# One subtraction of a fused transformer layer, issued by VectorE in place of GpSimd

## The chip, the core and the metric

The kernel is one program on one core of one Trainium2 chip. Its time is device microseconds (us) from the launch of the program to its end, as the chip reports it. Engines are named as the profile names them: PE is TensorE, PEld its weight loads, DVE VectorE, ACT ScalarE, POOL GpSimd, SP SyncE.

## What is computed

The reference is one layer with adaptive layer norm on a batch of 4 sequences of 1024 rows of 256 numbers: attention, then a routed feed-forward block. The part that the change touches is the last product of the feed-forward block.

```python
h = _layernorm(x) * (1 + ca) + sa
x = x + ga * attention(h)                  # 16 query heads, 4 key heads, causal
h = _layernorm(x) * (1 + cb) + sb
# feed-forward on h:
routed = sigmoid(h @ w_router + b_router) > 0.5
v = rmsnorm(h, norm1_w) @ wv + bv
g = h + v @ wo
h2 = rmsnorm(g, norm2_w)
mlp = (silu(h2 @ w_gate) * (h2 @ w_up)) @ w_down      # inner width FF = 704
x = x + gb * where(routed, g + mlp, h)
```

## The kernel before

The program handles the four sequences one after the other, but the work of neighbouring sequences is interleaved: a hand-written list of step names, ORDER, gives one common order of all steps, and each engine runs those steps of the list that are its own, in that order. An engine never takes a later step ahead of an earlier one. Steps that depend on each other over engines are tied by semaphores, one for each kind of step: a step raises the semaphore of its kind when it is done, and whoever needs it waits for the count. Where ORDER carries a digit behind a PE step, it is the PSUM bank which that step takes; eight banks are shared by all steps, and a PE step also waits until the former holder of its bank has been read out.

The feed-forward block works on pairs of row tiles (256 rows, four pairs to a sequence) and on inner blocks of 128. The 704 inner columns are five full blocks and one of 64, in three groups of two blocks: group 0, the middle group 1 (blocks 2 and 3), and group 2. For each pair and group the steps are

- gate and up on PE (lines 792 to 794), each into a bank;
- sil on ACT (L1001, or L1003 and L1004 for group 2): silu of gate;
- fft on DVE (L1255, or L1257 and L1259 for group 2): product of sil and up, in float32, into one of two buffers of 128x512;
- ffhi on ACT (L1015, or L1017 and L1018): the product rounded to the short format in which PE multiplies fast, the high word;
- the low word, the product less its high word, into fflo. For groups 0 and 2 it is step fflo on DVE (L1267; L1270 and L1272). For the middle group it is step ffl, one instruction of 128x512 on POOL (L564).

Then step down on PE (L581 to L583, 809, 810) multiplies the inner blocks with w_down in three passes: high by high, high by low, low by high. Before block 2 it waits for ffl, the low words of the middle group. Step sum (L1278) on DVE reads the result, and step fin on POOL (L573, L574) applies the gate and adds the residual.

Other steps that the text speaks of: hT, hhi and hlo transpose the normed rows on PE (L756), take the high words on ACT (L969) and the low words on DVE (L1226); a is the product with the fused v and router weights on PE (L581 to L583 with W1hi); route (L1236, L1237, L1239) on DVE reads it; h2T (L775) transposes for gate and up; max and mxr are the row maxima of the scores (PE L684, DVE L1165); ytm (L1189 to L1194) on DVE normalizes attention's output, and ynT (L736) on PE transposes it; rs1, rs2, rstd2 on POOL are inverse square roots (L481, L482); norm1 on POOL is L542, pmask L549.

There are 16 middle groups, one for each pair of each sequence. On the waiting side, these lines matter: the wait of down, and that of fft, which may write its buffer again only when the low word of two groups earlier is done.

```python
for f in range(FB):
    if f == GROUPS[LO_P][0]:
        wait("ffl", j + 1)
    elif f == GROUPS[NG - 1][0]:
        wait("fflo", j * (NG - 1) + 2)
```

Of the kernel before, what the change touches and what calls it, by code (L numbers as in the profile page):

```python
# [6 lines left out]
F32 = mybir.dt.float32  # L7
F32R = mybir.dt.float32r
BF16 = mybir.dt.bfloat16
ALU = mybir.AluOpType  # L10
# [51 lines left out]
NG = 3  # L62
# [5 lines left out]
GROUPS = [(0, 1), (2, 3), (4, 5)]  # L68
LO_P = 1
# [137 lines left out]
def adaln_layer(nc, x, Wq, bq, Wk, bk, Wv, bv, Wo, bo, w_router, b_router, n1, f_wv, f_bv, f_wo, n2,  # L207
                w_gate, w_up, w_down, c_in, wmod, rope_cos, rope_sin, out):
    ctx = ExitStack()
    with ctx:  # L210
# [99 lines left out]
        fft = sb("fft", [P, 2, CH])  # L310
# [9 lines left out]
        ffhi = sb("ffhi", [P, 2, NF, PAIR_T], F32R)  # L320
        fflo = sb("fflo", [P, 2, FB, PAIR_T], F32R)
# [34 lines left out]
        S = {n: sem("s_" + n) for n in N} | dict(setM=s_setM)  # L356
        N |= dict(setM=0)

        def flat(ap):
            return ap.rearrange("p k n -> p (k n)")  # L360
# [96 lines left out]
        @block.gpsimd  # L457
        def _(pool):
            pool.memset(ident[:], 0.0)
            pool.memset(mask_qk[:], 0.0)  # L460
            pool.memset(expo[:], -0.5)
            pool.memset(eps_ln[:], LN_EPS)
            pool.memset(eps_rms[:], RMS_EPS).then_inc(s_const, 1)
            pool.wait_ge(s_const, 1)
            pool.affine_select(out=ident[:], in_=ident[:], compare_op=ALU.not_equal, fill=1.0, base=0,
                               pattern=[[-1, P]], channel_multiplier=1)
            pool.affine_select(out=mask_qk[:], in_=mask_qk[:], compare_op=ALU.is_ge, fill=NEG, base=0,
                               pattern=[[-1, P]], channel_multiplier=1).then_inc(s_const, 1)
            pool.wait_ge(s_const, 2)
            pool.tensor_copy(ident_b[:], ident[:]).then_inc(s_const, 1)  # L470
            chained = [0]

            def then(i):

                i.then_inc(S["pchain"], 1)
                chained[0] += 1
                pool.wait_ge(S["pchain"], chained[0])

            def rsqrt(dst, src, eps, done):

                then(pool.tensor_tensor(dst, src, eps, ALU.add))  # L481
                pool.tensor_tensor(dst, dst, expo[:, 0:dst.shape[1]], ALU.pow).then_inc(done, 1)  # L482

            for kind, b, n, _ in STEPS:
                two = slice(2 * n, 2 * n + 2)
                ring = slice(2 * n % TPC, 2 * n % TPC + 2)

                def wait(name, k):
                    pool.wait_ge(S[name], b * N[name] + k)

                def earlier(name, k):
                    if b > 0:
                        pool.wait_ge(S[name], (b - 1) * N[name] + k)

                def over_two(row):
                    return row.unsqueeze(1).to_broadcast([P, 2, C])

                if kind == "pzero":
                    pool.memset(V[:], 0.0)
                    pool.memset(stk[:], 0.0).then_inc(s_const, 1)  # L500
                    pool.wait_ge(s_const, C_ZERO - 1)
                    pool.memset(stk[:, :, H:2 * H, QK:QKM], 1.0)
                    pool.memset(V[:, :, :, D:D + 1], 1.0).then_inc(s_const, 1)
                elif kind == "gmod":
                    pool.wait_ge(s_setM, M_MOD)
                    rows = modr.rearrange("b (v n) -> b v n", v=4)
                    gates = rows[:, 0:4:3, :]
                    pool.tensor_scalar(rows[:, 2, :], rows[:, 2, :], 1.0, 1.0, ALU.mult, ALU.add)
                    then(pool.tensor_scalar(gsgn, gates, 0.0, 2.0, ALU.is_ge, ALU.mult))
                    then(pool.tensor_scalar(gsgn, gsgn, 1.0, -1.0, ALU.mult, ALU.add))  # L510
                    then(pool.tensor_tensor(gabs, gsgn, gates, ALU.mult))
                    then(pool.tensor_scalar(gabs, gabs, 3.0e38, 0.25, ALU.min, ALU.max))
                    pool.tensor_tensor(gates, gsgn, gabs, ALU.mult).then_inc(s_gmod, 1)
                elif kind == "gw1":
                    pool.wait_ge(s_setM, M_W1 + 1)
                    pool.tensor_tensor(flat(W1lo[:]), flat(w1_st[:]), flat(W1hi[:]).bitcast(F32), ALU.subtract
                                       ).then_inc(s_w1, 1)
                elif kind == "gprep":

                    pool.wait_ge(s_setA, 2 * n + 3)  # L520
                    for src, k, blk, cols in pieces[n]:
                        hi = guhi[:, k, blk, cols]
                        i = pool.tensor_tensor(gulo[:, k, blk, cols], src.rearrange(
                            "p (f n) -> p f n", n=hi.shape[2]), hi.bitcast(F32), ALU.subtract)
                    i.then_inc(s_setG, 1)
                elif kind == "gwd":

                    pool.wait_ge(s_setA, 2 * PIECES + 2)
                    pool.tensor_tensor(wdlo[:], wd_st, wdhi[:].bitcast(F32), ALU.subtract).then_inc(s_setG, 1)
                elif kind == "rstd1":  # L530
                    wait("stats", n + 1)
                    earlier("norm1", (n + 1) * TPC)
                    ts = slice(n * TPC, (n + 1) * TPC)
                    then(pool.tensor_scalar(nmean[:, ts], mv1[:, ts, 0], -1.0, 0.0, ALU.mult, ALU.add))
                    rsqrt(rstd1[:, ts], mv1[:, ts, 1], eps_ln[:, ts], S["rstd1"])
                elif kind == "norm1":
                    wait("rstd1", n // TPC + 1)
                    if n >= TPC:
                        wait("xT", (n - TPC) // 2 + 1)
                    else:  # L540
                        earlier("xT", (NT + n - TPC) // 2 + 1)
                    pool.tensor_scalar(xn[:, n % TPC, :], xres[:, b % NX, n, :], nmean[:, n:n + 1], rstd1[:, n:n + 1],  # L542
                                       ALU.add, ALU.mult).then_inc(S["norm1"], 1)
                elif kind == "pmask":

                    u = DIAG[n]
                    wait("exp", 2 * (u + 1))
                    block_ = PT[:, u % 2, :, 0:P]
                    pool.affine_select(out=block_, in_=block_, compare_op=ALU.is_ge, fill=0.0, base=0,  # L549
                                       pattern=[[0, H], [1, P]], channel_multiplier=-1).then_inc(S["pmask"], 1)  # L550
                elif kind == "rstd2":
                    wait("x1", n + 1)
                    rsqrt(rstd2[:, two], mv2[:, two, 1], eps_ln[:, two], S["rstd2"])
                elif kind == "rs1":
                    wait("ms1", n + 1)
                    rsqrt(rs[:, 0, two], ms[:, 0, two], eps_rms[:, two], S["rs1"])
                elif kind == "rs2":
                    wait("ms2", 2 * n + 2)
                    rsqrt(rs[:, 1, two], ms[:, 1, two], eps_rms[:, two], S["rs2"])
                elif kind == "ffl":  # L560
                    m = n * NG + LO_P
                    wait("ffhi", m + 1)
                    blocks = slice(GROUPS[LO_P][0], GROUPS[LO_P][1] + 1)
                    pool.tensor_tensor(flat(fflo[:, n % 2, blocks, :]), fft[:, m % 2, :],  # L564
                                       flat(ffhi[:, n % 2, blocks, :]).bitcast(F32), ALU.subtract).then_inc(S["ffl"], 1)
                elif kind == "fin" and (b, n) == (B - 1, NJ - 1):
                    continue
                elif kind == "fin":
                    wait("sum", 2 * n + 2)
                    if n == 0:  # L570
                        pool.wait_ge(s_gate[b % 2], 16 * (b // 2) + 16)
                    z = zbuf[:, (b * NJ + n) % Z_PAIRS]
                    then(pool.tensor_tensor(z, z, over_two(gate_b[:, b % 2, :]), ALU.mult))  # L573
                    pool.tensor_tensor(xres[:, b % NX, two, :], xres[:, b % NX, two, :], z, ALU.add  # L574
                                       ).then_inc(S["fin"], 1)
# [446 lines left out]
        def _(dve):  # L1022
# [34 lines left out]
            for kind, b, n, _ in STEPS:  # L1057
                def wait(name, k):
                    dve.wait_ge(S[name], b * N[name] + k)
# [186 lines left out]
                elif kind == "fft":  # L1246
# [9 lines left out]
                    else:  # L1256
# [2 lines left out]
                        i = dve.tensor_tensor(fft[0:FR, n % 2, PAIR_T:CH], sil[FR:P, n % 2, PAIR_T:CH],  # L1259
                                              of("gate", b, n)[FR:P, PAIR_T:CH], ALU.mult)  # L1260
                    i.then_inc(S["fft"], 1)
                elif kind == "fflo":
                    j, g = n // (NG - 1), (0, NG - 1)[n % (NG - 1)]
                    m = j * NG + g
# [58 lines left out]
```

## Time and profile before

| what | value |
|---|---|
| median of 3 runs | 465.63 us |
| lowest and highest run | 465.51 and 466.37 us |
| span of the profiled execution | 466.8 us |
| granted clock of PE, mean of the span | 0.990 |
| PE busy | 437.2 us, 94% of the span |
| DVE busy | 353.9 us, 76% |
| ACT busy | 308.4 us, 66% |
| POOL busy | 182.2 us, 39% |

The profile is of one execution, with a span from its first to its last instruction of 466.8 us; the profile gives no other time of that execution. That span is 1.2 us over the median of the three timed runs, so differences are formed inside the profile and then put on the median. The clock was full but for short stretches at the start and the very end.

### The profile page before, as it was taken

The numbers are of one execution on the slowest core, as the hardware profiler recorded it, in microseconds if no ns is written. First come the engines' busy times: TensorE is split into PE (matmuls) and PEld (weight loads), VectorE is DVE, ScalarE is ACT, GpSimd is POOL, SyncE is SP. The second block draws the span as 40 slices with busy tenths as digits, with TensorE's granted clock in tenths as the row PEclk, the third lists the DMA queues.
The fourth block names the chain that finished last, engine by engine and source line by source line (L and its number), as shares of the span: only waits on it lengthen the run. The fifth ranks groups of instructions, "written<-read, shape, count | busy, mean of one in ns | idle before, by whom it ended". The sixth has DMA issues, their size and how long they took to land. (4 is left out here: it accounts for less than half of the span.)

```text
span 466.8 us, 9486 instructions
## 1 busy us (share of the span) xinstructions
PE 437.2 (94%) x3320; PEld 371.8 (80%) x3320; DVE 353.9 (76%) x796; ACT 308.4 (66%) x640; POOL 182.2 (39%) x262
## 2 busy tenths in 40 slices
PE   5887979888989999999999999999999999999996
PEld 5674545686587688997858999999898798999995
DVE  4579968788989488898855889888885766578565
ACT  2298578775588887527697764676768698645441
POOL 6376527410246220214827404523243333325622
PEclk9999899999999999999999999999999999999998
DMA  7921030000000100020021000000010000000001
GB/s 192 333 93 51 3 97 1 2 1 3 0 3 11 43 2 0 2 70 1 27 86 24 2 1 24 1 26 5 20 51 9 24 22 2 25 1 24 22 25 46
DMA packets 16576, 16.04 MB, mean 34 GB/s; under 512 B 4233, under 2 KB 14926, under 8 KB 16530
## 3 DMA queue, kind: packets, MB, share of 16 engines
q1 hardware_dynamic: 16530, 15.44, 10.8%
q8 instruction: 28, 0.46, 0.4%
q14 instruction: 18, 0.15, 0.1%
HBM read 11.09 MB, written 4.21 MB: 33 GB/s over the span
## 5 line engine op out<-in xcount | busy, mean ns | idle before, releaser
L792 PE MATMUL banks<-gTh,guhi 128*128 128x256 f32 x352 | 101.2, 287 | 0.0
L794 PE MATMUL banks<-gTh,gulo 128*128 128x256 f32 x352 | 98.8, 281 | 0.0
L793 PE MATMUL banks<-gTl,guhi 128*128 128x256 f32 x352 | 98.7, 280 | 0.0
L937 ACT ACTIVATE PT<-banks 128x1024 f32<-128x1024 f32 (+3 forms) x96 | 74.5, 810 | 29.8 <-PE banks L708 24.4
L792 PEld LDWEIGHTS banks<-gTh,guhi 128*128 128x128 f32 x352 | 66.4, 189 | 1.6 <-issue 0.7
L1165 DVE TENSOR_REDUCE mxp<-banks 128x2 f32<-128x1024 f32 (+3 forms) x56 | 61.9, 1141 | 6.4 <-PE banks L684 3.9
L793 PEld LDWEIGHTS banks<-gTl,guhi 128*128 128x128 f32 x352 | 66.5, 189 | 0.3
L794 PEld LDWEIGHTS banks<-gTh,gulo 128*128 128x128 f32 x352 | 66.4, 189 | 0.0
L684 PE MATMUL banks<-QKT 128*128 128x512 f32 (+3 forms) x192 | 49.9, 368 | 6.8 <-ACT QKT L915 3.4
L708 PE MATMUL banks<-QKT 128*128 128x512 f32 (+3 forms) x192 | 50.9, 369 | 0.9 <-ACT PT L937 0.4
L708 PEld LDWEIGHTS banks<-QKT 128*128 128x128 f32 x192 | 30.3, 190 | 23.3 <-issue 21.2
L581 PE MATMUL banks<-wdhi,ffhi 128*128 128x256 f32 x160 | 46.0, 287 | 0.0
L573 POOL TENSOR_TENSOR zbuf<-zbuf,gate_b 128x512 f32<-128x512 f32 x15 | 19.6, 1305 | 66.4 <-DVE zbuf L1278 66.4
L582 PE MATMUL banks<-wdlo,ffhi 128*128 128x256 f32 x160 | 45.1, 282 | 0.0
L583 PE MATMUL banks<-wdhi,fflo 128*128 128x256 f32 x160 | 45.1, 282 | 0.0
L684 PEld LDWEIGHTS banks<-QKT 128*128 128x128 f32 x192 | 29.6, 193 | 13.9 <-issue 7.2
L549 POOL TENSOR_SCALAR_AFFINE_SELECT PT<-PT 128x512 f32<-128x512 f32 x32 | 21.1, 660 | 49.7 <-ACT PT L937 49.5
L720 PE MATMUL banks<-PT,V 128*32 128x512 f32 (+3 forms) x384 | 38.6, 495 | 1.7 <-POOL PT L549 1.6
L481 POOL TENSOR_TENSOR rs<-ms,eps_rms 128x2 f32<-128x2 f32 x32 | 7.6, 239 | 70.1 <-ACT sq L974 51.1
L915 ACT ACTIVATE QKT<-banks 64x512 fp32r<-64x512 f32 (+1 forms) x48 | 26.6, 590 | 10.5 <-PE banks L673 10.1
L1001 ACT ACTIVATE sil<-banks 128x512 f32<-128x512 f32 x32 | 18.7, 594 | 22.3 <-PE banks L794 21.5
L564 POOL TENSOR_TENSOR fflo<-fft,ffhi 128x512 fp32r<-128x512 f32 x16 | 20.9, 1304 | 31.4 <-ACT ffhi L1015 31.4
(178 smaller groups left out, 1093.4 us busy)
## 6 DMA issues: line engine op xcount, KB each, us to landing
xres<-in_L_attn_x SPq DMA_DIRECT2D x8, 512.0 KB, 4.4
out_x<-xres SPq DMA_DIRECT2D x16, 256.0 KB, 2.1
wm_st<-in_L_wmod SPq DMA_DIRECT2D x1, 1024.0 KB, 7.9
modB<-mod_scratch SPq DMA_DIRECT2D x4, 256.0 KB, 3.4
wg_st<-in_L_ffn_w_gate SPq DMA_DIRECT2D x1, 704.0 KB, 5.0
wu_st<-in_L_ffn_w_up SPq DMA_DIRECT2D x1, 704.0 KB, 6.2
xres<-in_L_ffn_w_down SPq DMA_DIRECT2D x1, 640.0 KB, 5.7
wm_st<-in_L_wmod SPq DMA_DIRECT2D x1, 512.0 KB, 6.2
```

The source lines that it names most:

```text
L581: pe.matmul(o, hi, whi, start=first, stop=False)
L582: pe.matmul(o, hi, wlo, start=False, stop=False)
L583: return pe.matmul(o, lo, whi, start=False, stop=last)
L684: i = pe.matmul(o[:, e, m * kn:(m + 1) * kn], QKT[:, q, qt * P:(qt + 1) * P], QKT[:, 2 + 2 * q + e, k0:k0 + kn], start=(m == 0), stop=not ...
L708: i = pe.matmul(o[:, e, 0:CH - q0], QKT[:, 2 + 2 * q + e, j * P:(j + 1) * P], QKT[:, q, c * CH + q0:(c + 1) * CH], start=True, stop=True)
L720: i = pe.matmul(o[h * 2 * D:(h + 1) * 2 * D, q0:CH], V[:, j, h, :], PT[:, n % 2, h, 0:CH - q0], start=(j == 0), stop=(q0 == CH - P), skip_ ...
L792: pe.matmul(out_, guhi[:, k, blk, :], gh, start=(m == 0 and k == 0), stop=False)
L793: pe.matmul(out_, guhi[:, k, blk, :], gl, start=False, stop=False)
L794: i = pe.matmul(out_, gulo[:, k, blk, :], gh, start=False, stop=(m == len(blocks) - 1 and k == KB - 1))
L915: i = act.activation(QKT[rows, to, cols].rearrange("p q (t n) -> p q t n", t=2), o[rows, q:q + 2], ACT.Copy)
L937: act.activation(PT[:, u % 2, 2 * q:2 * q + 2, 0:CH - q0], both("prob", b, n)[:, :, 0:CH - q0], ACT.Exp, scale=float(D) ** -0.5).then_inc( ...
L1165: dve.tensor_reduce(dst, both("max", b, n)[:, :, 0:len(at) * kn].rearrange("p e (m k) -> p e m k", k=kn), AX.X, ALU.max).then_inc(S["mxr"], 1)
```

## The change

The subtraction of the middle group's low words has the same operands, the same semaphores and the same place in ORDER. It is taken out of POOL's program and put into DVE's.

```diff
@@ block.gpsimd @@
-                elif kind == "ffl":
-                    m = n * NG + LO_P
-                    wait("ffhi", m + 1)
-                    blocks = slice(GROUPS[LO_P][0], GROUPS[LO_P][1] + 1)
-                    pool.tensor_tensor(flat(fflo[:, n % 2, blocks, :]), fft[:, m % 2, :],
-                                       flat(ffhi[:, n % 2, blocks, :]).bitcast(F32), ALU.subtract).then_inc(S["ffl"], 1)
@@ block.vector @@
+                elif kind == "ffl":
+                    m = n * NG + LO_P
+                    wait("ffhi", m + 1)
+                    blocks = slice(GROUPS[LO_P][0], GROUPS[LO_P][1] + 1)
+                    dve.tensor_tensor(flat(fflo[:, n % 2, blocks, :]), fft[:, m % 2, :],
+                                       flat(ffhi[:, n % 2, blocks, :]).bitcast(F32), ALU.subtract).then_inc(S["ffl"], 1)
```

Six lines fewer stand ahead of DVE's code after the change, so its lines carry numbers lower by six (L1257 becomes L1251); the moved instruction is L1260. Two places of DVE's program show what stands around it. The first is the first sequence's first pair, some 138 us into the execution. DVE's rows before the change (in brackets the semaphores that a row waits for):

```order
L1221 SCALAR_TENSOR_TENSOR hbuf<-hbuf,rstd,modB 128x256
L1226 TENSOR_TENSOR hTl<-banks,hTh 128x512 [waits s_hhi]
L1257 TENSOR_TENSOR fft<-sil,banks 128x256 [waits s_up,s_fflo,s_sil]
L1259 TENSOR_TENSOR fft<-sil,banks 64x256
L1189 RECIPROCAL rc<-banks 128x16 [waits s_ynT,s_yT]
```

And DVE's rows of the same place after it:

```order
L1215 SCALAR_TENSOR_TENSOR hbuf<-hbuf,rstd,modB 128x256
L1220 TENSOR_TENSOR hTl<-banks,hTh 128x512 [waits s_hhi]
L1260 TENSOR_TENSOR fflo<-fft,ffhi 128x512 [waits s_ffhi]
L1251 TENSOR_TENSOR fft<-sil,banks 128x256 [waits s_up,s_fflo,s_sil]
L1253 TENSOR_TENSOR fft<-sil,banks 64x256
L1183 RECIPROCAL rc<-banks 128x16 [waits s_ynT,s_yT]
```

The subtraction, with its wait for ffhi, now stands between hlo and the fft of group 2.

The second place is the last sequence's second pair, some 433 us in. DVE's rows before:

```order
L1270 TENSOR_TENSOR fflo<-fft,ffhi 128x256 [waits s_ffhi]
L1272 TENSOR_TENSOR ffhi<-fft,ffhi 64x256
L1226 TENSOR_TENSOR hTl<-banks,hTh 128x512 [waits s_hhi]
L1278 SCALAR_TENSOR_TENSOR zbuf<-banks,r_yes,zbuf 128x256 [waits s_down] x3
L1244 TENSOR_TENSOR gTl<-banks,gTh 128x512 [waits s_h2hi]
```

And after:

```order
L1270 TENSOR_TENSOR fflo<-fft,ffhi 128x256 [waits s_ffhi]
L1272 TENSOR_TENSOR ffhi<-fft,ffhi 64x256
L1220 TENSOR_TENSOR hTl<-banks,hTh 128x512 [waits s_hhi]
L1260 TENSOR_TENSOR fflo<-fft,ffhi 128x512 [waits s_ffhi]
L1278 SCALAR_TENSOR_TENSOR zbuf<-banks,r_yes,zbuf 128x256 [waits s_down] x3
L1238 TENSOR_TENSOR gTl<-banks,gTh 128x512 [waits s_h2hi]
```

Here it stands behind the low words of group 2 and of hT, and ahead of three sums.

On POOL, at the first place, before the change:

```order
L482 TENSOR_TENSOR rs<-rs,expo 128x2 [waits s_pchain]
L542 TENSOR_SCALAR xn<-xres,nmean,rstd 128x256 [waits s_xT,s_rstd1]
L564 TENSOR_TENSOR fflo<-fft,ffhi 128x512 [waits s_ffhi]
L542 TENSOR_SCALAR xn<-xres,nmean,rstd 128x256 [waits s_xT,s_rstd1]
L481 TENSOR_TENSOR rs<-ms,eps_rms 128x2 [waits s_ms1]
```

After it, the two norm1 instructions follow each other:

```order
L482 TENSOR_TENSOR rs<-rs,expo 128x2 [waits s_pchain]
L542 TENSOR_SCALAR xn<-xres,nmean,rstd 128x256 [waits s_xT,s_rstd1] x2
L481 TENSOR_TENSOR rs<-ms,eps_rms 128x2 [waits s_ms1]
```

PE's and ACT's programs, and all DMAs, are the same.

## Rows read from the trace of the kernel before

**Rows 1.** Busy time of each engine by stretch, us (instructions), then clock and DMA.

```profile
130.00:464.00 334.00, 328.37 (x2633) 292.37 (x2632) 252.92 (x556) 225.08 (x474) 124.21 (x167) 1.00 0.07 20
```

**Rows 2.** The tile fflo: who writes it; duration ns min/median/max, first and last start.

```profile
L1267 DVE TENSOR_TENSOR fflo<-fft,ffhi x16: 679/688/1801, 132.2 to 453.0; 128x512 fp32r<-128x512 f32 x16
L564 POOL TENSOR_TENSOR fflo<-fft,ffhi x16: 1277/1292/1443, 140.2 to 453.8; 128x512 fp32r<-128x512 f32 x16
```

**Rows 3.** Timeline, first pair: start us, us, engine, line, [idle before <-releaser].

```profile
137.26 0.69 DVE L1226 TENSOR_TENSOR hTl<-banks,hTh 128x512 fp32r<-128x512 f32 x1 [0.35 <-ACT hTh L969]
137.87 0.41 DVE L1257 TENSOR_TENSOR fft<-sil,banks 128x256 f32<-128x256 f32 x1
138.29 0.42 DVE L1259 TENSOR_TENSOR fft<-sil,banks 64x256 f32<-64x256 f32 x1
138.38 0.64 ACT L1015 ACTIVATE ffhi<-fft 128x512 fp32r<-128x512 f32 x1
139.04 0.28 PE L581 MATMUL banks<-W1hi,hTh 128*128 128x258 f32 x1
```

**Rows 4.** Timeline, second sequence, third pair.

```profile
297.43 0.69 POOL L482 TENSOR_TENSOR rstd<-rstd,expo 128x2 f32<-128x2 f32 x1
297.57 0.68 DVE L1267 TENSOR_TENSOR fflo<-fft,ffhi 128x512 fp32r<-128x512 f32 x1
298.31 0.61 ACT L1015 ACTIVATE ffhi<-fft 128x512 fp32r<-128x512 f32 x1
299.14 1.23 DVE L1165 TENSOR_REDUCE mxp<-banks 128x2 f32<-128x1024 f32 x1 [0.89 <-PE banks L684]
301.09 0.27 PE L775 MATMUL banks<-ident,hbuf 128*128 128x128 f32 x1
```

**Rows 5.** Timeline, third sequence, third pair.

```profile
385.48 0.22 DVE L1236 TENSOR_SCALAR r_yes<-banks,brout 128x1 f32<-128x1 f32 x1 [0.18 <-PE banks L583]
386.13 0.48 DVE L1239 SCALAR_TENSOR_TENSOR zbuf<-dl,r_yes,hbuf 128x256 f32<-128x256 f32 x1
386.21 0.62 ACT L1015 ACTIVATE ffhi<-fft 128x512 fp32r<-128x512 f32 x1
387.69 0.28 PE L581 MATMUL banks<-W1hi,hTh 128*128 128x258 f32 x1
```

**Rows 6.** Timeline, last sequence, second pair.

```profile
428.44 1.29 POOL L564 TENSOR_TENSOR fflo<-fft,ffhi 128x512 fp32r<-128x512 f32 x1 [0.77 <-ACT ffhi L1015]
432.81 0.28 PE L581 MATMUL banks<-wdhi,ffhi 128*128 128x256 f32 x1
432.85 0.69 DVE L1226 TENSOR_TENSOR hTl<-banks,hTh 128x512 fp32r<-128x512 f32 x1
```

**Rows 7.** Timeline: POOL subtractions beside DVE: the first, the sixth, and the last such DVE instruction.

```profile
140.18 1.44 POOL L564 TENSOR_TENSOR fflo<-fft,ffhi 128x512 fp32r<-128x512 f32 x1
140.41 1.50 DVE L1270 TENSOR_TENSOR fflo<-fft,ffhi 128x256 fp32r<-128x256 f32 x1
...
410.67 1.35 POOL L564 TENSOR_TENSOR fflo<-fft,ffhi 128x512 fp32r<-128x512 f32 x1 [0.66 <-ACT ffhi L1015]
410.91 1.39 DVE L1194 TENSOR_TENSOR ytm<-ytm 128x256 f32<-128x256 f32 x1
412.45 0.30 PE L736 MATMUL banks<-ident,ytm 128*128 128x128 f32 x1 [0.34 <-DVE ytm L1194]
...
445.55 1.80 DVE L1267 TENSOR_TENSOR fflo<-fft,ffhi 128x512 fp32r<-128x512 f32 x1
```

**Rows 8.** Waits of PE from 130 to 464 us: total, times, longest.

```profile
PE banks L746 <- DVE hTl L1226: 0.4, 1, 0.4
PE banks L736 <- DVE ytm L1194: 0.3, 1, 0.3
PE banks L708 <- DVE mxp L1165: 0.2, 1, 0.2
PE banks L684 <- DVE mxp L1165: 0.2, 1, 0.2
```

## The prediction

> **What bounds the kernel now.** I read the table of stretches first. Between 130 and 464 us, which is where all 16 middle groups fall, PE is busy for 328.4 of 334.0 us at the full clock [rows 1]. The reader is to see two things there. PE is the bound, with 5.6 us of idle time in all, so nothing that merely frees another engine can give more than a part of that. And because PE has hardly any idle time, a wait that is forced on PE is not made up later: its cost stays in the total. DVE is busy for 252.9 us of the same stretch, POOL for 124.2, ACT for 225.1 [rows 1]. DVE thus has 81 us of slack on average, and the change asks for some 11. An average says nothing about the place, however. So the question is what each of the 16 moved instructions holds up at the place where it lands, and I went through the timeline around each, with the list of who waits on whom at hand. The list of PE's waits gives the other side: of PE's waits in the stretch, those that DVE ended come to 1.1 us where a DVE instruction near a POOL subtraction is what was late [rows 8].
>
> **What is removed and added.** Removed are 16 POOL instructions of 1.29 us (median), 20.7 us of POOL time; added are 16 DVE instructions. DVE has the very same form already, for group 0, at 0.69 us (median) [rows 2]: 16 x 0.69 = 11.0 us of DVE. PE, ACT and the DMAs issue what they did. The low words of a group are ready in 0.69 us instead of 1.29, but only from the time at which DVE comes to them.
>
> **What hides it and what does not.** The instruction waits for ffhi. On POOL nobody of importance stood behind that wait. On DVE everything that follows in its order stands behind it. Where ffhi is long done and the next DVE instruction is itself waiting for PE, the cost is nothing, and for twelve of the sixteen places I find that or nearly that: the DVE idle time there, or PE's distance to the result, covers 0.69 us. Four places are not covered. Two hand-overs are counted in each: from ytm to PE it took 0.15 us (410.91 + 1.39 = 412.30, PE at 412.45) [rows 7], and I take 0.05 for the one from ACT to DVE. Back to back, DVE's instructions overlap by 0.08 us (137.26 + 0.69 = 137.95 against a start at 137.87) [rows 3].
>
> First pair. DVE is free at 137.95, but ffhi ends only at 138.38 + 0.64 = 139.02. The subtraction runs from 139.07 to 139.76, so fft of group 2 starts at 139.68 instead of 137.87, 1.81 late. Its second half ended at 138.71 and now ends at 140.52. PE's step a at 139.04 takes the bank that this fft frees, and starts at 140.67: **1.6 us** [rows 3].
>
> Second sequence, third pair. ffhi ends at 298.31 + 0.61 = 298.92; the subtraction ends at 299.66, the group 0 subtraction behind it (0.68, formerly at 297.57) at 300.26, and the row maximum starts at 300.18 instead of 299.14, 1.04 late. It ended at 300.37 and now ends at 301.41. PE's transposes at 301.09 want its bank: 301.56, **0.5 us** [rows 4].
>
> Third sequence, third pair. ffhi ends at 386.83, the subtraction at 387.57, and route starts at 387.49 instead of 385.48, 2.0 late. It ended at 386.61, now at 388.62; PE's step a at 387.69 takes a bank that route frees: 388.77, **1.1 us** [rows 5].
>
> Last sequence, second pair. Here POOL had finished at 428.44 + 1.29 = 429.73, three microseconds ahead of PE's down at 432.81. DVE gets there after hlo, at 433.46 (hlo ends at 433.54), and ends at 434.15: PE restarts at 434.30, **1.5 us** [rows 6].
>
> These four make 1.6 + 0.5 + 1.1 + 1.5 = 4.7 us. For the other twelve I add 0.4: several have a margin of a few tenths only (the backlog of DVE after the third place, the next pair at 397 us, the row maxima at 202 us). This is a choice between 0 and 12 x 0.69 = 8.3; it lies near the low end because by the timeline ffhi had ended 3 to 10 us earlier in all but one of them, and DVE waits for PE soon after (these are too many rows to show). Sum of the costs: 5.1 us.
>
> **What it gives back.** While POOL's subtraction runs, a DVE instruction that reads two operands from SBUF is held until it ends. At 140.41 a DVE instruction of 128x256 took 1.50 us; the sixth of them, ytm at 410.91, took 1.39; the last, of 128x512, took 1.80 at 445.55 where its median is 0.69 [rows 2, 7]. I count seven so lengthened, by 0.2 to 1.1 us, 5.5 us in all. So DVE's net load grows by 11.0 - 5.5 = 5.5 us only. Of this, PE sees what it waited for behind them: 0.4 at 146 us, 0.2 at 214 us, 0.2 at 319 us, 0.3 at 412 us, 1.1 us [rows 8]. All four come behind a delay of PE itself and vanish if DVE is not late by as much. I take them in full. POOL is off the path otherwise, and its freed 20.7 us I cost at nothing: what it does next mostly waits for DVE or ACT.
>
> The Trainium skill says in "SBUF — State Buffer", section "Who interferes with whom", that a DVE instruction with two SBUF inputs contends with any GpSimd instruction that reads SBUF, whichever comes first holding the shared pair for its whole length. The stretched rows agree. But the small POOL inverse root at 297.43 to 298.12 did not hold the DVE subtraction that started at 297.57 and took 0.68 [rows 4], so here the rule holds for the wide POOL instructions alone. By the rule taken literally the new subtraction at the third place would also wait for POOL's small operations, half a microsecond more; by the row it does not.
>
> Net: 5.1 - 1.1 = +4.0 us. The profiled execution's span of 466.8 would become 470.8; on the median of the timed runs, 465.63, it is **469.6 us**, 0.9% slower.
>
> **The rivals.** (1) The release of the shared port outweighs the waits: faster. For it speaks that the seven stretched instructions alone hold 5.5 us and that two of them stand right in front of a wait of PE. If the four places cost nothing, the time is 465.6 - 1.1 = 464.5. It decides when the four places together cost under 0.9 us; the last one alone is put at 1.5 by rows that leave no cover, so I give it 0.07. (2) It is hidden: the waits cost no more than the 1.1 us that come back, 465.6 within 0.9. It needs PE's order to have margins that I misread, for instance that ACT's ffhi comes earlier at two of the places. 0.08. (3) DVE becomes the bound in stretches: the new wide instructions meet POOL's own wide ones (gate and residual of step fin, the masks) and are themselves held up to 1.1 us, as the row at 445.55 was, and each delay of DVE pushes the ones behind. Three of sixteen such hits on places that PE waits for, with half of the other twelve insertions showing, give 4.0 + 3 x 0.7 + 6 x 0.3 = 7.9, so 473.5. Against it: DVE still idles for 70 us of the stretch. 0.12. (4) The forecast, +2 to +6.5 us: 0.73.
>
> **How the numbers follow.** The likeliest case is the sum, 469.6. Its low end leaves one of the two large places unpaid (4.0 - 1.6 = 2.4, 468.0), its high end grants nothing back and one collision on the path (5.1 + 1.1 = 6.2, 471.8). To hold 8 in 10 I reach a little into the hidden case and into rival 3: 467.3 to 472.4. A difference under 0.2%, 0.9 us, is about what a measurement of this kernel cannot tell from none. Slower: 0.73 + 0.12 and the part of rival 2 above 0.2%, 0.86; same 0.07; faster 0.07.
>
> **What the changed profile would show.** L1260 on DVE 16 times, median 0.69 us, three of them after an idle time that ACT's ffhi ended (places one, two, three). PE idle before a step a near 139 us by 1.6, ended by DVE's fft; near 302 by 0.5; near 389 by 1.1, ended by route; near 436 by 1.5, ended by L1260 itself. PE idle in the stretch up from 5.6 to some 10 us, with busy time of PE unchanged. ytm back at 0.43 us and the wait of 0.3 behind it gone. DVE busy some 5 to 6 us more, not 11. I am wrong if these waits of PE are missing; if DVE's busy time rises by 11 or more, the port gives nothing back and rival 3 is near; if PE's waits appear but the time doesn't follow, the trace's bound was another than PE.

## The result and the profile after

The changed kernel takes 472.01 us (median of 6 runs, 471.03 to 473.87), the kernel before 465.67 us in the same measurement. The ratio of their runs is 1.0127, 95% interval 1.0109 to 1.0144: 5.1 to 6.7 us slower.

From the page of the changed kernel, its span and the busy times of its engines:

```profile
span 470.2 us, 9486 instructions
PE 436.5 (93%) x3320; PEld 370.9 (79%) x3320; DVE 359.9 (77%) x812; ACT 308.1 (66%) x640; POOL 161.4 (34%) x246
```

DVE is busy 6.0 us more (353.9 before), POOL 20.8 us less, PE as long as before. The spans themselves (466.8 and 470.2) differ by only 3.4 us, because the execution of before that was profiled began slowly: its first 130 us, which the change does not touch, took 1.9 us longer than those of the changed kernel. So all traces are compared below over one stretch that leaves the start out: from the start of the matmuls behind PE's wait for a mask near 130 us to the start of the last residual addition on DVE. First PE's row that opens it, then DVE's row that closes it, of before:

```profile
134.29 0.42 PE L720 MATMUL banks<-PT,V 128*32 128x128 f32 x8 [0.97 <-POOL PT L549]
463.78 0.42 DVE L1287 TENSOR_TENSOR xres<-xres,zbuf 128x256 f32<-128x256 f32 x1
```

And of the changed kernel:

```profile
132.36 0.42 PE L714 MATMUL banks<-PT,V 128*32 128x128 f32 x8 [0.96 <-POOL PT L549]
467.11 0.42 DVE L1287 TENSOR_TENSOR xres<-xres,zbuf 128x256 f32<-128x256 f32 x1
```

That is 329.49 us before and 334.75 us after, +5.26 us. This is inside the interval of the timed runs.

The table of stretches of the changed kernel, the row that answers to [rows 1]:

```profile
130.00:468.00 338.00, 326.93 (x2617) 290.73 (x2615) 257.21 (x564) 223.72 (x472) 103.03 (x151) 1.00 0.06 20
```

By this window PE's idle time is 338.0 - 326.9 = 11.1 us where it was 5.6, but the window reaches 0.9 us beyond the last residual addition (467.11), where that of [rows 1] reaches 0.2 us. Over the stretch that the marks above bound, first of before and then of the changed kernel:

```profile
134.29:463.78 329.49, 325.04 (x2601) 289.63 (x2601) 249.09 (x544) 221.60 (x468) 121.44 (x164) 1.00 0.07 20
132.36:467.11 334.75, 325.53 (x2601) 289.92 (x2601) 254.99 (x560) 221.40 (x468) 100.67 (x148) 1.00 0.06 20
```

The same 2601 matmuls run at the full clock in both. PE's idle time goes from 4.45 to 9.22 us, +4.8, and its busy time grows by 0.5: the loss is for the most part idle time of PE. Who ended it is in the list of PE's waits from 130 to 468 us, of the changed kernel, as far as DVE ended them (total, times, longest):

```profile
PE banks L575 <- DVE fft L1253: 1.4, 1, 1.4
PE banks L691 <- DVE mt L1173: 1.4, 1, 1.4
PE banks L575 <- DVE fflo L1260: 1.4, 1, 1.4
PE banks L575 <- DVE zbuf L1233: 0.9, 1, 0.9
PE banks L740 <- DVE Wo_l L1090: 0.8, 1, 0.8
PE banks L769 <- DVE fft L1253: 0.5, 1, 0.5
PE banks L769 <- DVE mxp L1159: 0.3, 1, 0.3
```

The wait for Wo_l, 0.8 us, is in the list of before too. The other six are new and make 6.0 us; all four waits of [rows 8] are gone. The rows of the timeline at five of the six, the ones that the prediction spoke of (the fourth is the pair at 397 us that it named in passing):

```profile
138.73 0.36 PE L575 MATMUL banks<-W1hi,hTh 128*128 128x258 f32 x1 [1.45 <-DVE fft L1253]
300.21 0.30 PE L769 MATMUL banks<-ident,hbuf 128*128 128x128 f32 x1 [0.29 <-DVE mxp L1159]
388.93 0.36 PE L575 MATMUL banks<-W1hi,hTh 128*128 128x258 f32 x1 [0.93 <-DVE zbuf L1233]
401.59 0.30 PE L769 MATMUL banks<-ident,hbuf 128*128 128x128 f32 x1 [0.55 <-DVE fft L1253]
436.04 0.39 PE L575 MATMUL banks<-wdhi,ffhi 128*128 128x256 f32 x1 [1.40 <-DVE fflo L1260]
```

The chain at the first place, of the changed kernel, answers to [rows 3]: DVE idles 1.10 us until ffhi is there, and fft of group 2 follows the subtraction.

```profile
136.46 0.64 ACT L1009 ACTIVATE ffhi<-fft 128x512 fp32r<-128x512 f32 x1
...
137.13 0.69 DVE L1260 TENSOR_TENSOR fflo<-fft,ffhi 128x512 fp32r<-128x512 f32 x1 [1.10 <-ACT ffhi L1009]
137.74 0.41 DVE L1251 TENSOR_TENSOR fft<-sil,banks 128x256 f32<-128x256 f32 x1
138.16 0.42 DVE L1253 TENSOR_TENSOR fft<-sil,banks 64x256 f32<-64x256 f32 x1
```

What the port gives back is seen at ytm, which took 1.39 us before [rows 7]. In the changed kernel no POOL instruction runs beside it, and PE does not wait behind it:

```profile
413.14 0.42 DVE L1188 TENSOR_TENSOR ytm<-ytm 128x256 f32<-128x256 f32 x1
```

The sixth new wait is the one that the prediction did not name. DVE and POOL around it, in the changed kernel:

```profile
343.26 1.06 DVE L1260 TENSOR_TENSOR fflo<-fft,ffhi 128x512 fp32r<-128x512 f32 x1
344.24 0.17 DVE L1166 TENSOR_REDUCE mx<-mxp 128x16 f32<-128x32 f32 x1
344.45 1.12 DVE L1170 TENSOR_SCALAR mt<-mx 128x8 fp32r<-128x8 f32 x2
345.61 1.30 DVE L1173 SCALAR_TENSOR_TENSOR mt<-mx,mt 128x8 fp32r<-128x8 f32 x2
...
343.14 0.64 POOL L549 TENSOR_SCALAR_AFFINE_SELECT PT<-PT 128x512 f32<-128x512 f32 x1 [9.74 <-ACT PT L931]
343.75 1.73 POOL L567 TENSOR_TENSOR zbuf<-zbuf,gate_b 128x512 f32<-128x512 f32 x1
345.55 1.26 POOL L568 TENSOR_TENSOR xres<-xres,zbuf 128x512 f32<-128x512 f32 x1
...
347.06 0.30 PE L691 MATMUL banks<-ident,mt 128*128 128x128 f32 x1 [1.40 <-DVE mt L1173]
```

And the same place in the kernel before:

```profile
344.97 0.28 DVE L1176 TENSOR_SCALAR mt<-mx 128x8 fp32r<-128x8 f32 x2
345.29 1.22 DVE L1179 SCALAR_TENSOR_TENSOR mt<-mx,mt 128x8 fp32r<-128x8 f32 x2
...
345.13 1.28 POOL L573 TENSOR_TENSOR zbuf<-zbuf,gate_b 128x512 f32<-128x512 f32 x1
...
346.88 0.27 PE L697 MATMUL banks<-ident,mt 128*128 128x128 f32 x1
```

This is step mneg, small instructions in a chain that ends in a transpose on PE. Before, its first two (L1176) had both started when POOL's gate multiplication began at 345.13, and the pair behind them was held. After the change the subtraction stands in front. It is itself held by POOL's mask step (pmask, L549), 1.06 us and not 0.69. The pair behind it then falls into the gate multiplication, 1.12 us and not 0.28, and the next pair into POOL's residual addition, 1.30. The insertion of 0.69 us makes PE wait 1.4 us, after the 0.3 us of margin that it had (the chain ended at 346.51, PE started at 346.88).

The list of waits understates what each place costs. It counts from the modelled end of the matmul before, some 0.28 us after that one's start, while matmuls of this kind that wait for nothing start every 0.12 us. So the table compares starts. It takes the 2601 matmuls of the stretch in order; the lag of one is its start behind PE's opening row in the changed kernel, less the same in before. The step is the change of the lag from one matmul to the next, for all steps of more than 0.1 us.

| PE start before | PE start after | first matmul of | step, us |
|---|---|---|---|
| 139.04 | 138.73 | a, first place | +1.61 |
| 146.18 | 145.44 | product with Wo, behind hlo | -0.52 |
| 147.84 | 146.87 | a | -0.16 |
| 214.49 | 213.28 | scores (L702) | -0.39 |
| 301.09 | 300.21 | h2T, second place | +0.44 |
| 318.73 | 317.41 | row maxima (L678) | -0.36 |
| 346.88 | 347.06 | transpose behind mneg | +1.55 |
| 387.69 | 388.93 | a, third place | +1.09 |
| 399.37 | 401.59 | h2T, the pair at 397 us | +0.70 |
| 412.45 | 414.16 | ynT, behind ytm | -0.50 |
| 432.81 | 436.04 | down, fourth place | +1.56 |

The six costs make 6.95 us, the five gains 1.93 us. Steps of 0.1 us and less, spread over the stretch, make the other 0.24 of the 5.26 us. Such steps repeat from kernel to kernel: the first is 1.61 or 1.62 us in all five traces that have it, and the gains of 0.39, 0.36 and 0.50 us come out the same in the traces of all kernels in which POOL issues no wide subtraction at those places.

### The profile page after: what moved, and what is told of

It is laid out like the page before. It is cut to its first block and busy times, and to the rows that moved or that the text cites. A ratio compares the mean times of both kernels' runs of the same rounds, so it can differ in the third digit from the quotient of the medians.

```text
span 470.2 us, 9486 instructions
## 1 busy us (share of the span) xinstructions
PE 436.5 (93%) x3320; PEld 370.9 (79%) x3320; DVE 359.9 (77%) x812; ACT 308.1 (66%) x640; POOL 161.4 (34%) x246
## 5 line engine op out<-in xcount | busy, mean ns | idle before, releaser
L678 PE MATMUL banks<-QKT 128*128 128x512 f32 (+3 forms) x192 | 50.3, 371 | 6.6 <-ACT QKT L909 3.4
L702 PE MATMUL banks<-QKT 128*128 128x512 f32 (+3 forms) x192 | 50.6, 368 | 0.7 <-ACT PT L931 0.4
L702 PEld LDWEIGHTS banks<-QKT 128*128 128x128 f32 x192 | 29.9, 189 | 23.0 <-issue 20.8
L678 PEld LDWEIGHTS banks<-QKT 128*128 128x128 f32 x192 | 29.8, 195 | 13.6 <-issue 6.9
L549 POOL TENSOR_SCALAR_AFFINE_SELECT PT<-PT 128x512 f32<-128x512 f32 x32 | 20.8, 650 | 56.5 <-ACT PT L931 56.3
L575 PEld LDWEIGHTS banks<-wdhi,ffhi 128*128 128x128 f32 x160 | 30.1, 188 | 1.9 <-DVE fflo L1260 1.6
```

Of the source, the lines that this page charges most:

```text
L575: pe.matmul(o, hi, whi, start=first, stop=False)
L678: i = pe.matmul(o[:, e, m * kn:(m + 1) * kn], QKT[:, q, qt * P:(qt + 1) * P], QKT[:, 2 + 2 * q + e, k0:k0 + kn], start=(m == 0), stop=not ...
L702: i = pe.matmul(o[:, e, 0:CH - q0], QKT[:, 2 + 2 * q + e, j * P:(j + 1) * P], QKT[:, q, c * CH + q0:(c + 1) * CH], start=True, stop=True)
```

## The experiments

Each was timed beside the kernel before on its chip. The column "stretch" is the one defined above, from each kernel's own trace, as a difference to before's 329.49 us; the ratio is that of the timed runs to the kernel before.

| kernel | stretch, us | ratio, 95% interval |
|---|---|---|
| changed kernel | +5.26 | 1.0127 (1.0109 to 1.0144) |
| five moved | +0.55 | 1.0008 (0.9986 to 1.0030) |
| six moved | -1.05 | 0.9976 (0.9948 to 1.0005) |
| short on VectorE | +2.61 | 1.0064 (1.0035 to 1.0092) |
| short on GpSimd | -1.26 | 0.9959 (0.9933 to 0.9985) |
| GpSimd still reads | +7.64 | 1.0178 (1.0118 to 1.0238) |
| last place alone | +1.33 | 1.0028 (1.0002 to 1.0054) |
| six places alone | +6.72 | 1.0126 (1.0069 to 1.0183) |
| ten places alone | -1.36 | 0.9971 (0.9937 to 1.0005) |
| eleven, one moved | -1.77 | 0.9979 (0.9961 to 0.9996) |
| mneg place moved | +3.81 | 1.0111 (1.0076 to 1.0146) |

The medians of the kernel before lay at 466.4 to 467.3 us in these measurements, so the expectations, which are given in microseconds on 465.7, are read as differences. One profile stands behind each stretch, so its scatter from one execution to the next is not measured; with the start left out, it agrees with the ratio's interval in all rows of the table. Several of these intervals are wider than the effects in question. Where the text sets apart causes that differ by less, it goes by the trace alone.

**Moving the subtraction within VectorE's order.** Same work on the same engine; only its place in the common order differs.

```diff
+MOVED = {(0, 0): ('ytm', 1, 0), (1, 2): ('mxr', 3, 6), (2, 2): ('fflo', 2, 4),
+         (2, 3): ('fft', 2, 11), (3, 1): ('fft', 3, 5)}
+def replaced(order):
+    out = [s for s in order if not (s[0] == "ffl" and s[1:3] in MOVED)]
+    for (b, n), behind in MOVED.items():
+        at = [s[:3] for s in out].index(behind)
+        out.insert(at + 1, ("ffl", b, n, None))
+    return out
-STEPS = steps()
+STEPS = replaced(steps())
```

> All 16 subtractions stay on VectorE; five of them (first pair; second sequence, third pair; third sequence, third and fourth pair; last sequence, second pair) are moved in the order to just behind the step that TensorE waits for (or, in the last case, to where their high word is ready and VectorE idle). Theory A, the waits at single places: TensorE's waits there, 1.45 + 0.29 + 0.93 + 0.55 + 1.40 = 4.6 us in the changed kernel's trace, vanish, so 472.0 - 4.6 = 467.4 us, within 0.8. Rival B, VectorE's load: 11 us more work on VectorE cost wherever they stand, so moving them changes little: 471 to 472 us.

The stretch fell by 4.7 us against the changed kernel (4.6 expected). Of PE's six new waits one is left, the one at mneg. In the list of PE's waits that DVE ended, of this kernel:

```profile
PE banks L706 <- DVE mt L1188: 1.4, 1, 1.4
PE banks L755 <- DVE Wo_l L1105: 0.8, 1, 0.8
```

Rival B, the load, expected no change and falls: DVE does all the work that it does in the changed kernel.

The sixth, at mneg, was moved in addition, `(2, 0): ('mneg', 3, 1)`.

> As the kernel with five moved, and the subtraction of the third sequence's first pair also moved, behind the negated row maxima (mneg) in front of which it stood. Theory A: the wait of 1.40 us of TensorE at 347 us goes too, so 1.2 to 1.4 us less than with five moved: 466.1 us. Rival B, the load: no change against five moved. Rival C, collision only: the subtraction behind mneg meets the same wide GpSimd instructions, and the 1.4 us come back as another wait: no change either, but with VectorE instructions stretched behind mneg instead.

Another 1.6 us went, and the kernel is 1.05 us under before in the stretch, with all 16 subtractions on VectorE. Rival C, that the collision would only come back further on, falls for PE. In this kernel's trace the subtraction behind mneg took 0.68 us; it started first and lengthened POOL's residual addition to 1.77 us, but no wait of PE came of it. Moved alone in the changed kernel, the same place was tried again:

> The changed kernel with one subtraction moved, the third sequence's first pair, from in front of the negated row maxima (mneg) to behind them. Its own work is 0.69 us and TensorE had 0.3 us of margin before. Theory A with the collision: the whole wait of 1.40 us at 347 us goes, and the stretch from the mask to the end is 1.4 to 1.5 us shorter than the changed kernel's. Rival F, only its work counted: 0.4 us shorter.

The stretch is 1.45 us shorter than the changed kernel's. Rival F (0.4) counted the work only; the other microsecond is the collision. This goes by the trace: the timed ratios, 1.0111 and 1.0127, do not set the two kernels apart.

**Wait and work apart.** The changed kernel, with the subtraction cut to 2 columns from the third on:

```diff
+                    cols = slice(0, CH if b == 0 and n < 2 else 2)
-                    dve.tensor_tensor(flat(fflo[:, n % 2, blocks, :]), fft[:, m % 2, :],
-                                       flat(ffhi[:, n % 2, blocks, :]).bitcast(F32), ALU.subtract).then_inc(S["ffl"], 1)
+                    dve.tensor_tensor(flat(fflo[:, n % 2, blocks, :])[:, cols], fft[:, m % 2, cols],
+                                       flat(ffhi[:, n % 2, blocks, :]).bitcast(F32)[:, cols], ALU.subtract).then_inc(S["ffl"], 1)
```

> The changed kernel, but from the third subtraction on only 2 of the 512 columns are subtracted (low words of the middle group otherwise stay those of the first two pairs): the wait for the high word stays, the work of 0.69 us goes. Theory A: each of the six waits of TensorE shrinks by the 0.63 us of work or to nothing, except the first (still whole): 1.45 + 0 + 0.2 + 0.3 + 0 + 0.77 = 2.7 of 6.0 us stay, so 472.0 - 3.3 = 468.7 us. Rival B, load alone: with the load gone the time is that of the kernel before or under it, 464.5 to 465.7 us.

Measured +2.6 us in the stretch, ratio 1.0064, which is 3.0 us. PE's waits of this kernel:

```profile
PE banks L575 <- DVE fft L1253: 1.5, 1, 1.5
PE banks L691 <- DVE mt L1173: 1.0, 1, 1.0
PE banks L740 <- DVE Wo_l L1090: 0.8, 1, 0.8
PE banks L575 <- DVE fflo L1261: 0.7, 1, 0.7
PE banks L575 <- DVE zbuf L1233: 0.4, 1, 0.4
```

The first, third and last of the new ones are as expected; the load rival (464.5 to 465.7) is out. The miss is again mneg: 1.0 us where I had 0.2. There the timeline shows the collision with next to no work in it:

```profile
342.06 0.53 DVE L1261 TENSOR_TENSOR fflo<-fft,ffhi 128x2 fp32r<-128x2 f32 x1
342.52 0.17 DVE L1166 TENSOR_REDUCE mx<-mxp 128x16 f32<-128x32 f32 x1
342.73 1.20 DVE L1170 TENSOR_SCALAR mt<-mx 128x8 fp32r<-128x8 f32 x2
343.97 1.32 DVE L1173 SCALAR_TENSOR_TENSOR mt<-mx,mt 128x8 fp32r<-128x8 f32 x2
```

An instruction of 2 columns, which takes 0.13 to 0.16 us at the other places, is held to 0.53 us by the mask, and that is enough to push both pairs behind it into POOL's two wide instructions. So at mneg some 1.0 of 1.4 us is lost to being a little late, not to the 0.69 us of work.

**What GpSimd's silence gives.** The kernel before, with the subtraction on GpSimd cut in the same way:

> The kernel before, with the subtraction on GpSimd cut to 2 of 512 columns from the third on (low words of the middle group otherwise stay those of the first two pairs). It shows what freeing the shared port and GpSimd gives with nothing added to VectorE. Theory A: the waits of TensorE behind stretched VectorE instructions at 214, 319 and 412 us go, 0.2 + 0.2 + 0.3, the one at 146 us stays: 465.0 us. Rival D, the port does not matter to TensorE: 465.7 us. Rival E, the port matters everywhere: 464 us or less.

The waits at 214, 319 and 412 us went as expected and the one at 146 stayed (0.4, behind the second of the two whole ones). The stretch is 1.26 us shorter, where 0.7 was expected, the sum of the three waits. The starts of PE's matmuls account for the rest: the three steps are -0.39, -0.36 and -0.50, together -1.25 us, and no other step exceeds 0.1 us. The counterpart adds reads to GpSimd in the changed kernel:

```diff
+        idle = sb("idle", [P, CH])
...
+                elif kind == "ffl":
+                    wait("ffhi", n * NG + LO_P + 1)
+                    if b == 0 and n == 0:
+                        pool.wait_ge(s_setG, weights_split)
+                    then(pool.tensor_tensor(idle[:], flat(guhi[:, 0, 0:4, :]).bitcast(F32),
+                                       flat(gulo[:, 0, 0:4, :]).bitcast(F32), ALU.subtract))
```

> The changed kernel, and GpSimd in addition subtracts two constant 128x512 pieces of the gate weights into an unused tile, at the place and behind the high word where it made the subtraction before (its result is used by nobody). VectorE's added work and GpSimd's reads of SBUF are then both there. Theory A, the port gives back what the short subtraction on GpSimd showed (1.3 us from the mask at 130 us to the end): it is taken away again, so 1 to 2 us above the changed kernel, 473 to 474 us, with VectorE instructions stretched by up to 1.1 us under the extra GpSimd ones. Rival D, GpSimd's reads do not matter to the end: 472.0 us.

2.4 us over the changed kernel in the stretch, a little over the range of 1 to 2. The intervals of the two ratios overlap (1.0118 to 1.0238 with four runs, against 1.0109 to 1.0144), so the sign rests on the trace. Both engines can lose in turn, as at the second place (L1267 is the moved subtraction here, L1274 that of group 0):

```profile
299.06 1.80 POOL L565 TENSOR_TENSOR idle<-guhi,gulo 128x512 f32<-128x512 f32 x1 [0.88 <-ACT ffhi L1016]
...
299.01 0.69 DVE L1267 TENSOR_TENSOR fflo<-fft,ffhi 128x512 fp32r<-128x512 f32 x1 [1.31 <-ACT ffhi L1016]
299.62 1.78 DVE L1274 TENSOR_TENSOR fflo<-fft,ffhi 128x512 fp32r<-128x512 f32 x1
...
302.69 0.30 PE L776 MATMUL banks<-ident,hbuf 128*128 128x128 f32 x1 [1.39 <-DVE mxp L1166]
```

DVE's subtraction starts first and POOL's is held for 0.5 us; POOL's then holds DVE's next one until it ends. PE's wait there is 1.39 and not 0.29 us. In the stretch DVE is busy 4.7 us more than in the changed kernel (259.68 against 254.99) with the same instructions on DVE. The run gives POOL its time back together with its reads and cannot part the two; what speaks for the reads is that PE's waits come behind lengthened DVE instructions. By the starts of PE's matmuls, the gains of 0.36 and 0.50 us are gone (that of 0.39 stays), and the second and third place cost 1.54 and 1.40 us where they cost 0.44 and 1.09. Rival D, that GpSimd's reads do not matter, falls.

**The places apart.** A set of pairs says which engine takes which subtraction; both engines have the code and skip what is the other's.

```diff
+ON_DVE = {(3, 1)}
...
                 elif kind == "ffl":
+                    if (b, n) not in ON_DVE:
+                        continue
```

> The kernel before, with the subtraction of one single group (last sequence, second pair) on VectorE and the other 15 on GpSimd. Theory A: TensorE waits 1.40 us in down for it near 434 us, and nothing else changes: 1.4 us over the kernel before, 467.1 us. Rival B, VectorE's load: one instruction of 0.69 us costs at most 0.7 us, 465.7 to 466.4.

+1.33 us for one instruction of 0.69 us, in the place where down waits for it. The load rival, at most 0.7, falls by the trace; the ratio's interval, 0.1 to 2.5 us, still holds it. Its rows:

```profile
430.83 0.68 DVE L1271 TENSOR_TENSOR fflo<-fft,ffhi 128x512 fp32r<-128x512 f32 x1
...
431.57 0.38 PE L584 MATMUL banks<-wdhi,ffhi 128*128 128x256 f32 x1 [1.23 <-DVE fflo L1271]
```

> The six subtractions at which TensorE was seen waiting in the changed kernel's trace are on VectorE, the other ten on GpSimd as before. Theory A: all of the cost and little of the gain: waits of 1.45 + 0.29 + 1.40 + 0.93 + 0.55 + 1.40 = 6.0 us, less 0.4 at 146 us that is then covered: 5.6 us over the kernel before, 471.3 us. Rival B, the load: six sixteenths of the 6.3 us, 468.1 us.

+6.7 us in the stretch, +5.9 by the ratio: six subtractions on VectorE cost all that the sixteen do, and more, since the port gives back nothing here but at 146 us (PE's waits for mxp and ytm behind POOL's subtraction are all still in its trace). Theory A had 5.6, the load 2.4. By the starts of PE's matmuls the six places cost 6.77 us here and 0.69 comes back near 146 us, which makes 6.1; the expectation was added up from the list of waits, which understates each. The last 0.6 us comes in steps of about 0.1 us and less, and stays open.

> The complement: the ten other subtractions on VectorE, the six on GpSimd. Theory A: no cost, and the gain of the port at the four places from 170 us on where GpSimd held VectorE: 0.7 to 1.3 us under the kernel before, 464.4 to 465.0 us. Rival B, the load: ten sixteenths of the 6.3 us above it, 469.6 us.

-1.4 us in the stretch: the other ten cost nothing, and give the port's gain (-0.39, -0.36 and -0.50 at the places of PE's old waits). The ratio's interval just includes no change and is far from the load rival's +0.8%. The two sets add up, 6.72 - 1.36 = 5.36 against 5.26 for the whole change.

The best version keeps the ten, adds the first pair's behind ytm, and leaves five on GpSimd, `ON_DVE` being the ten and (0, 0), with `MOVED = {(0, 0): ('ytm', 1, 0)}`.

> The ten subtractions that cost nothing on VectorE, and the first pair's as well but moved behind attention's normalization (ytm), so that GpSimd's stretch of VectorE at 140 us goes too; the other five stay on GpSimd. Theory A: what the ten gave (1.35 us from the mask at 130 us to the end) and the wait of 0.4 us at 146 us besides: 1.7 us under the kernel before in that stretch, 0.4% of the time. Rival B, the load: over the kernel before.

-1.77 us in the stretch; ratio 0.9979, interval 0.9961 to 0.9996, so it is faster than the kernel before by 0.2 to 1.8 us, and faster than the change by some 7. In its trace no wait of PE that DVE ended is left but Wo_l, which the change does not touch.

## Why the prediction was right, and where it was short

The forecast was 469.6 us, in a range of 467.3 to 472.4; 472.01 was measured, 0.4 us below its upper end. The sign and the mechanism held. The difference was put at +4.0 us and is 5.3 in the stretch, 5.1 to 6.7 by the ratio. The sum of it, term by term, beside the steps of PE's starts:

| term | forecast, us | measured, us |
|---|---|---|
| the four places | +4.7 | +4.70 |
| the other twelve | +0.4 | +2.25 |
| given back | -1.1 | -1.93 |
| steps of 0.1 us and less | 0 | +0.24 |
| sum | +4.0 | +5.26 |

- *PE is the bound and keeps every wait.* Shown: over the stretch its idle time grew by 4.8 us and its busy time by 0.5, and the stretch by 5.3.
- *The four places*, 1.6 + 0.5 + 1.1 + 1.5 = 4.7. The steps are 1.61 + 0.44 + 1.09 + 1.56 = 4.70, each within 0.1 of its forecast. In the list of waits they are 1.45 + 0.29 + 0.93 + 1.40 = 4.1. The experiments that moved these and the pair at 397 us, and the last one alone, show them to be the cause.
- *"For the other twelve I add 0.4."* This is the term that was mis-sized most. One of the twelve, in front of mneg, cost 1.55 us by itself, and the pair at 397 us, which I had named as short of margin, 0.70. I had read the place of mneg for margins and for ffhi, which had been ready for 7 us, and not for what runs on POOL at the moment. This is the mechanism of rival 3 (new instructions meeting POOL's wide ones), to which I gave 0.12. It struck once, and with a multiplied price, because the instructions that it pushed fell into POOL's too. The other ten places together cost nothing that shows (ten places alone).
- *What it gives back*, 1.1. All four waits of [rows 8] are gone, but they gave back 1.93 us. I had summed the list of waits, which counts from the modelled end of the matmul before and so leaves out 0.1 to 0.2 us at each; the rest came at 146 us, where the matmuls at 147 us also start 0.16 us earlier. Adding GpSimd's reads again took 0.9 of it away; the other 1.5 us of that run is new cost, for the most part at the second and third place.
- *Luck in the sum.* The two errors, +1.85 and -0.83, have opposite signs. With the gain as forecast, and all else as measured, the kernel would have lain 0.8 us higher and so above the range. That the time fell inside it does not vouch for the term of the twelve.
- *DVE's net load*, +5.5: busy time rose by 6.0. The size was right, and it is beside the point: the load costs nothing (ten places alone, five and six moved). Rival 1, the release outweighing the waits, is true of the same sixteen instructions once they are placed elsewhere, in the stretch (-1.05 us); by the ratio that gain is not clear of zero (0.9948 to 1.0005).
- *The small POOL instructions at the third place*, at which I put no hold by [rows 4]: the subtraction started at 387.05 inside POOL's inverse root (386.85 to 387.54) and took 0.69 us. Rightly left out.

## What to carry to other kernels

An engine with a quarter of its time free can still be the wrong one: price a moved instruction at each place where it lands, by what it waits for, what stands behind it and who waits for that, not by the load that it adds. In a fixed order the engine and the place are one decision; the change was a loss of 1.3% with the place kept and a gain of about 0.2% with six places changed or avoided. Before putting work in front of a chain of small VectorE instructions, look at what GpSimd runs at that moment, since being half a microsecond late can cost one wide GpSimd instruction after the other.

## What the runs showed of the hardware

A wide GpSimd instruction holds back more of VectorE than instructions with two SBUF operands. In the changed kernel at 344.45 a pair of tensor_scalar instructions with a single SBUF source, 128x8, took 1.12 us beside POOL's gate multiplication where it takes 0.28 us otherwise. The Trainium skill covers this in "SBUF — State Buffer", section "Who interferes with whom", by which tensor_scalar can enter a mode that takes both of DVE's ports, when its operands allow it. The hold in the trace agrees with that; no run here shows which ports the instruction used. The hold goes by who starts first and passes on: with GpSimd's reads added, DVE's 0.69 us lengthened POOL's instruction to 1.80 us (1.29 is usual), and that lengthened DVE's next to 1.78 (0.69 is usual). Small POOL instructions did not do so: in the trace of before, none of the DVE instructions with two SBUF operands that started inside one of POOL's inverse roots (128x2 or 128x4) was lengthened by more than 0.05 us, as in [rows 4].
